# Routing in groups of three, three and two rows, the first a lap sooner, and an opening in another order

## The reference, cut to what matters

```
# 1. encoder, d = 128
x = emb[tokens]; x = x + scan(x @ W_upd + b)(decay, mask = token != 0) @ W_f + b_f
x = ln(x) * g + b
for i in range(4): x = x + gelu(ln(x) @ W1[i] + b1[i]) @ W2[i] + b2[i]
h = x @ head_W + head_b                                   # 64 wide
# 2. linear attention on layernorm(h), 4 heads of 32, softmax of k over the sequence, of q over 32
h = h + rmsnorm((context @ softmax(q)) @ w_out + b_out) * g_out + layernorm(h)
# 3. mixture of 8 experts on layernorm(h) (a second layernorm inside)
logits = xn @ Wr + br                                     # 8 wide
w = softmax of the two largest logits, 0 for the other six (first index wins a tie)
h = h + layernorm... + sum_e w_e * (gelu(xn @ W1[e] + b1[e]) @ W2[e] + b2[e])
```

## Time and profile before

| what | us |
|---|---|
| median of 3 runs | 427.89 (425.44 to 429.58) |
| profiled execution, own time | 426.03 |
| its span, first to last instruction | 424.2 |
| mean granted TensorE clock | 0.991 |
| busy: PE / DVE / ACT / POOL | 388.5 / 351.3 / 326.5 / 269.2 |
| VectorE idle for ScalarE's high parts in the layers | 25.2 |
| DMA, mean | 35 GB/s |

### The profile page before, as it was taken

One profiled execution on the slowest core, in us unless ns is written; L12 is line 12 of the kernel. 1 busy time (PEld: TensorE's weight loads), 2 busy tenths in 40 slices (PEclk: granted clock), 3 DMA queues, 4 the chain that ended last, 5 costly groups with the idle time before them and its releaser, 6 DMA issues.

```text
span 424.2 us, 6301 instructions
## 1 busy us (share of the span) xinstructions
PE 388.5 (92%) x1977; PEld 312.4 (74%) x1977; DVE 351.3 (83%) x820; ACT 326.5 (77%) x558; POOL 269.2 (63%) x435
## 2 busy tenths in 40 slices
PE   4797879999999999999999989888887988999995
PEld 2586568888888888888888868677665756776883
DVE  3888689888898889888889889888777779989885
ACT  1254588999999998888977854667866989988994
POOL 0555787778777879778776556686434666435452
PEclk9699999999999999999999999999999999999999
DMA  6800011232212221222221000000000000000001
GB/s 211 338 2 0 1 24 29 50 51 51 40 35 51 50 53 26 50 51 50 37 39 50 2 0 2 1 2 2 0 0 2 0 2 13 12 15 12 14 13 25
DMA packets 15849, 14.94 MB, mean 35 GB/s; under 512 B 9796, under 2 KB 10568, under 8 KB 15560
## 3 DMA queue, kind: packets, MB, share of 16 engines
q1 hardware_dynamic: 15816, 14.54, 13.9%
HBM read 13.42 MB, written 1.11 MB: 34 GB/s over the span
## 4 chain that ended last, share of the span: by engine, by line
PE 63%; DVE 17%; ACT 13%; issue 4%; POOL 2%; DMA 1%; SPq 0%; DVEq 0%; ACTq 0%
PE ps L1439 56%; PE ps L1462 4%; ACT hid L869 4%; ACT w_all L875 3%; ACT ezf L804 2%; DVE hid L1381 2%; DVE hh L1232 1%; DVE stats L949 1%; PE ps L1470 1%; DMA xn<-in_w_f 1%; DVE x L1381 1%; ACT scratch L865 1%; ACT scratch L769 1%; ACT hid_lo L825 1%; DVE xn_lo L1388 1%
## 5 line engine op out<-in xcount | busy, mean ns | idle before, releaser
L683 ACT ACTIVATE hid<-ps,b_fold 128x512 f32<-128x512 f32 x128 | 84.0, 681 | 21.2 <-PE ps L1439 20.8
L1023 DVE TENSOR_TENSOR hid_lo<-hid,hid_hi 128x1024 fp32r<-128x1024 f32 x64 | 78.6, 1228 | 25.4 <-ACT hid_hi L688 25.2
L1439 PE MATMUL ps<-xn_hi,w_all 128*128 128x512 f32 x256 | 87.5, 403 | 0.6 <-DVE xn_lo L1018 0.6
L1439 PE MATMUL ps<-hid_hi,w_all 128*128 128x512 f32 x256 | 85.0, 393 | 0.0
L688 ACT ACTIVATE hid_hi<-hid 128x1024 fp32r<-128x1024 f32 x64 | 67.9, 1061 | 2.0
L1439 PEld LDWEIGHTS ps<-xn_hi,w_all 128*128 128x128 f32 x256 | 48.4, 189 | 10.8 <-issue 0.9
L1439 PEld LDWEIGHTS ps<-hid_hi,w_all 128*128 128x128 f32 x256 | 48.1, 188 | 9.9
L1439 PE MATMUL ps<-xn_lo,w_all 128*128 128x512 f32 x128 | 49.9, 390 | 0.0
L1439 PE MATMUL ps<-hid_lo,w_all 128*128 128x512 f32 x128 | 49.8, 389 | 0.0
L869 ACT ACTIVATE hid<-ps,eb_fold 128x512 f32<-128x512 f32 x64 | 44.1, 688 | 0.2
L1439 PE MATMUL ps<-hid_hi,ew 128*128 128x512 f32 x128 | 41.8, 409 | 1.1 <-ACT hid L869 0.8
(11 more groups left out here) (229 smaller groups left out, 895.6 us busy)
## 6 DMA issues: line engine op xcount, KB each, us to landing
rstd_row<-roots SPq DMA_DIRECT2D x29, 256.0 KB, 4.1
hh<-in_tokens SPq DMA_DIRECT2D x8, 256.0 KB, 7.8
hid<-in_w SPq DMA_DIRECT2D x1, 1024.0 KB, 7.1
rstd_row<-in_w SPq DMA_DIRECT2D x1, 1024.0 KB, 10.2
out<-hh SPq DMA_DIRECT2D x7, 128.0 KB, 2.0
ew_raw<-in_expert_w SPq DMA_DIRECT2D x1, 512.0 KB, 9.9
roots<-rstd SPq DMA_DIRECT2D x29, 2.0 KB, 1.4
ew_raw<-in_expert_w SPq DMA_DIRECT2D x1, 256.0 KB, 10.0
```

What stands on the lines that cost most here:

```text
L683: act.activation(hid[:, j % 2, f, :], bank[f], ACT.Gelu, bias=b1_fold[:, j // B * F + f:j // B * F + f + 1]).then_inc(gelu_done, 1)
L1023: dve.tensor_tensor(hid_lo[:, j % 2, 2 * p:2 * p + 2, :], hid[:, j % 2, 2 * p:2 * p + 2, :], hid_hi[:, j % 2, 2 * p:2 * p + 2, :].bitcast( ...
L1439: return pe.matmul(out, lhsT, rhs, start=start, stop=stop)
```

## The change

Groups become rows 0 to 2, 3 to 5, 6 and 7. Group 0's logits and first maximum move from lap -2 to the end of lap -3, the rest to lap -2, its gates are turned and copied in lap -1 ahead of the context of row 7 (with a wait for the queries and values, whose banks they use). Groups 1 and 2 have their hots and second maximum in units 4, 6 and 7 of laps 1 and 3, weights and gates in units 1 and 2 of the lap behind, and every later row's gates are turned and copied a unit later. In the opening, one-hot of row 7 goes to POOL, three broadcasts move ahead of bias and expert products, and twelve matmuls of the clock-keeping kind are added.

```diff
-POOL_ROWS = (3, 4, 5)
+POOL_ROWS = (3, 4, 5, 7)
-GROUPS = ((0, 4), (4, 2), (6, 2))
-GROUP_OF = (0, 0, 0, 0, 1, 1, 2, 2)
+GROUPS = ((0, 3), (3, 3), (6, 2))
+GROUP_OF = (0, 0, 0, 1, 1, 1, 2, 2)
@@ POOL, opening
-            for n in POOL_ROWS:
+            for n in POOL_ROWS[0:3]:
                 one_hot(n)
             pool.wait_ge(mhalf_set, 1)
             inverse_root_of_pair(0)
+            one_hot(POOL_ROWS[3])
             inverse_root_of_pair(2)
@@ ScalarE, attention laps
                 if c >= 0:
                     k_turned(c, c % 2)
+                if m == -1:
+                    copy_gates(0)
                 if a < B:
                     exp_k(a, a % 2)
-                if m == -1:
-                    act.preload_act_table(ACT.Gelu)
...
                 if a + 2 < B:
                     z_hi(a + 2, a % 2)
-                if m == -1:
+                if m == -2:
+                    act.preload_act_table(ACT.Gelu)
                     gate(0)
...
-                if m == -1:
-                    copy_gates(0)
                 if a < B:
                     copy_v(a, a % 2)
@@ ScalarE, expert loop
-                if u == 3 and m in (2, 4):
-                    gate(m // 2)
-                if u == 5 and m + 1 < B:
+                if u == 7 and m in (1, 3):
+                    gate((m + 1) // 2)
+                if u == 6 and m + 1 < B:
                     copy_gates(m + 1)
@@ VectorE, opening
-                if n in (2, 3):
-                    one_hot(n + 4)
+                if n == 2:
+                    one_hot(6)
@@ VectorE, attention laps: first_hot, second_max, second_hot, weights and gates_out of group 0
-                if m == -1:
+                if m == -2:
...
+                if m == -3:
+                    take_logits(0)
                 if m == -2:
-                    take_logits(0)
-                if m == -1:
                     v = weights(0, v)
                     gates_out(0, v)
-                if m == -2:
+                if m == -3:
                     v = first_max(0)
@@ VectorE, expert loop, laps 1 and 3
                     if u == 3:
                         v = first_max(p)
+                    if u == 4:
+                        v = first_hot(p, v)
+                    if u == 6:
+                        v = second_max(p, v)
+                    if u == 7:
+                        v = second_hot(p, v)
@@ VectorE, expert loop, laps 2 and 4
-                    if u == 0:
-                        v = first_hot(p, v)
+                    if u == 1:
+                        v = weights(p, v)
                     if u == 2:
-                        v = second_max(p, v)
-                    if u == 3:
-                        v = second_hot(p, v)
-                    if u == 5:
-                        v = weights(p, v)
-                    if u == 6:
                         gates_out(p, v)
@@ TensorE, opening
             look_up(1)
+            keep_clock_at(0, bank[5])
+            keep_clock_at(0, bank[5])
...
                 if n + 1 < B:
                     look_up(n + 1)
+                if n in (4, 5):
+                    broadcast(n - 4, n - 4)
                 if n <= 4:
                     keep_clock_at(n, bank[5])
...
                 if 3 <= n < 3 + L:
                     bias_fold(n - 3)
+                if n == 6:
+                    broadcast(3, 3)
...
-                if n in (4, 5, 6):
-                    broadcast((0, 1, 3)[n - 4], (0, 1, 3)[n - 4])
...
                     turn(x[:, n - 5, :], x0_ready, n - 4, place_ffn(n - 5))
+                if n in (5, 6):
+                    keep_clock_at(n, bank[5])
@@ TensorE, turn_gates
+                if b == 0:
+                    pe.wait_ge(qsub_ready, B)
+                    pe.wait_ge(v_ready, B)
@@ TensorE, attention laps
                 if c >= 0:
                     k_transposes(c, c % 2)
+                if m == -1:
+                    turn_gates(0)
...
                     hidden(1)
-                    turn_gates(0)
                 if a + 1 < B:
                     queries_and_values(a + 1, (a + 1) % 2)
-                if m == -2:
+                if m == -3:
                     logits(0)
@@ TensorE, expert loop
-                if u == 4 and m + 1 < B:
+                if u == 5 and m + 1 < B:
                     turn_gates(m + 1)
```

More of the change, by code:

```diff
@@ L1478, in look_up @@
                 else:
-                    pe.wait_ge(onehot_dve, 1 + n - len(POOL_ROWS) * (n > POOL_ROWS[0]))
+                    pe.wait_ge(onehot_dve, sum(k not in POOL_ROWS for k in range(n + 1)))
                 if n >= 2:
```

## The result

The changed kernel is slower: 429.68 us at the median of 21 runs (426.99 to 432.72) against 426.45 for the kernel before in 21 runs beside it (425.36 to 430.99). The ratio is 1.0061, with a 95% interval of 1.0039 to 1.0083, so about +2.6 us; the two medians are 3.2 apart. The forecast was -1.6 us. The profiled executions differ by more, 428.0 against 424.2 us of span: +3.8. TensorE's mean granted clock in them is 0.987 and 0.991.

A forecast was written before the change was run, and what follows sets the result against it. TensorE was taken as the bound, with VectorE full in laps 2 and 4. Opening -0.5, lap 3 at +0.4 (attention's -0.5 included), laps 3 and 4 -1.5 gave -1.6 us: 426.3 from the median 427.89, range 422.5 to 430.2.

The forecast's parts named there:

- Opening: Before the layers: broadcast wait removed, VectorE free for the transposes, full clock possibly held; -0.3 to -0.7 us, taken as -0.5.
- signs of being wrong: Laps 1 and 2 together changing by more than 2 us, or layers starting over 1 us sooner or later than 46.95.
- End of attention: Up to the first expert job: new 3.4 us VectorE wait, yet job at 323.0 instead of 323.58; -0.5 us (-0.9 to +0.5).
- TensorE's new waits: End of attention: waits for queries and values of row 7 were claimed to end before the gates do.
- Laps 1 and 2: Expert loop: earlier routing of rows 3 to 5 costs +1.4 us on lap 1's chain, 0.5 recovered in lap 2.
- Stalls I priced in: Lap 1: steps waiting out POOL's 1.29 us subtraction; chain +0.85 us without stalls, +2.9 with two, taken as +1.4.
- Laps 3 and 4: Expert loop: 2.05 us of VectorE steps for rows 6 and 7 move into lap 3; gain 0 to 3.0, taken as 1.5.
- work for both laps: Laps 3 and 4: VectorE's work sums to 20.9 us without stalls, 23.9 with three, against 23.83 taken.
- Rival 1: Expert loop: every routing step at an even unit waits out POOL's subtraction; +1.4 to +2.4, 429.3 to 430.3 us; chance 0.20.
- the six steps it named: Routing steps predicted to stall beside POOL: units 4 and 6 of laps 1 and 3, unit 2 of laps 2 and 4.
- Rival 3: End of attention: VectorE's 3.4 us wait not recovered, first job 2.5 us later, rest as forecast; 429.4 us; chance 0.08.
- Lap -1's own slack is 2.06: End of attention: argument against the rival that VectorE's new 3.4 us wait is not recovered.

The follow-up runs named there:

- e1: Kernel before with only the opening's edits (one-hot of row 7 on POOL, three broadcasts earlier, twelve clock-keeping matmuls): 426.1 us, ratio to before 0.9956.
- e2: Changed kernel with the opening of before, so the routing edits alone: 429.22 us, ratio to before 1.0046.
- e14: Kernel before with only the opening's moves (one-hot and broadcasts), without the added clock-keeping matmuls: 426.37 us, ratio to before 1.0010.
- e5: Kernel before with only the expert loop's new placement of routing steps, groups of four, two and two kept: 428.19 us, ratio to before 1.0038.
- e3: Changed kernel with twelve more clock-keeping matmuls in lap -2, filling TensorE's pause of 3.25 us: 428.69 us, ratio to before 1.0043.
- e10: Changed kernel with second_max and second_hot of rows 3 to 5 behind row 7's output and moments in lap 1: 431.83 us, ratio to before 1.0067.
- e6: Changed kernel with the expert loop's routing steps moved off the even units: 429.76 us, ratio to before 1.0048.
- e11: Changed kernel with the edits of e4, e9 and e10 together: 426.91 us, ratio to before 0.9995.
- e7: Changed kernel with the edits of e4 and e6 together: 427.61 us, ratio to before 1.0002.
- e8: Kernel before with the opening's edits and its own late routing moved to odd units of laps 2 and 4: 426.53 us, ratio to before 0.9995.
- e9: Changed kernel with the routing of rows 6 and 7 put back into lap 4: 429.34 us, ratio to before 1.0041.
- e4: Changed kernel with group 0's take_logits, first_max and first_hot moved behind the subtraction of lap -2: 427.0 us, ratio to before 0.9986.
- e13: Kernel before with only the opening's added clock-keeping matmuls, without the moves: 427.44 us, ratio to before 1.0021.

## Why the prediction was wrong

The change was to save 1.6 us and costs 2.6. The absolute forecast of 426.3 stood on the first three runs of the kernel before, whose median (427.89) is 1.4 above that of 21 runs; that the median of 429.68 lies inside the range of 422.5 to 430.2 is luck of that base.

**Opening, forecast -0.5.** Right in kind, but smaller: the clock held, VectorE's broadcast wait went, the transposes kept their place. In the profiled pair it is -0.2 from the tables on (-0.4 with e1). It also tripped one of my signs of being wrong, since the layers began 1.06 us sooner; 0.86 of that is the tables. The clock was at 0.50 from 14.1 to 20.9, longer than the 14.3 to 20.1 I had read. By the Trainium skill (TensorE: Matmul & The Clock Gate, What's actually happening) the six matmuls keep the full clock, since activity releases the throttle. The traces agree: none of the 12 profiled executions with them falls at 14, and three of the four without them do (before, e2 and e14; e5 does not). They don't keep it for long: e3 and e10 fell at 31 to 36 and e6 at 21 to 25.

**End of attention, forecast -0.5, measured +3.2.** The new wait is 3.31 us where I wrote 3.4, and the moments of lap -2 were done at 313.1, sooner than my 314.2. The step that failed is "TensorE's new waits (for queries and values of row 7) end before the gates do". I followed VectorE's queue and costed TensorE's idle time at nothing, since the gates came later, and I named another wait than the one that came. The masked context of row 6, 5.9 us behind the late addition in that queue, holds TensorE for 3.25 us, and what TensorE did next ran at half clock for 10.2 us: 2.7 us in this execution, by e3, and 0 to 0.5 in the four other profiled executions with the same pause. Had the clock held, 303.34 + 19.73 = 323.07 would have been the first job, and my 323.0 with it. Even that is luck and hides an error of about 1 us, since my number was made for an opening that ended 1.06 later: counted from the layers' start it is +0.5 at full clock (e3), where I forecast -0.5. The wait alone costs more, 2.0 us (e3 against e11); the new grouping wins 1.5 of them back. The earlier trace rows had shown me a pause and a drop in the opening, and I didn't ask what a new pause of the same size would do elsewhere.

**Laps 1 and 2, forecast +0.9, measured +0.96.** The number is right, and one part of its chain: TensorE's wait on row 7's output grew from 0.44 to 1.39. In part it is luck: lap 1 grew by 2.2 us and lap 2 fell by 1.3, where I expected lap 1 "a little longer" and 0.5 recovered in lap 2. Stalls I priced in are there (1.25 and 0.74 us for first_hot and second_max). What they cost isn't shown: e6 and e7, with these two gone and others left, take 0.5 us less.

**Laps 3 and 4, forecast -1.5, measured +0.53.** Lap 4 came to 11.28, as I said (near 11). Lap 3 came to 13.08, where I said 11.5. The step that failed is "work for both laps: 2 x 8.35 + 4.2 = 20.9 without stalls": it adds up VectorE alone. The column beside it in the earlier trace rows has TensorE busy 10.18 of 10.18 and 13.07 of 13.65, which leaves 0.58 us to gain in both laps, whatever VectorE does, unless TensorE's work moves to another lap. (e8 gained 0.60 there, and paid 1.3 in lap 2.) I had called VectorE the full engine of lap 4, 13.10 of 13.65; TensorE stood 0.03 behind it. Moving VectorE's steps from lap 4 to lap 3 moved TensorE's work the same way. e5 shows it with the old groups (24.33), and e9, which puts the steps back, gets 0.2.

**The rivals.** Rival 1 gave 429.3 to 430.3, and the median is 429.68. That is in part luck of the base: as a difference it gave +1.4 to +2.4, and it allowed 1.0 at most for the end of attention, which came to +3.2 in the profile. Five of the six steps it named were stretched (1.25 and 0.74 in lap 1, 0.91 and 1.01 in lap 3, 0.72 in lap 4); the sixth, in unit 2 of lap 2, took 0.25, and one it did not name took 1.36. Whether they cost the +1.5 us of the loop stays open: e8, with no stall, gained nothing, and in e7 a stall of 1.30 stands in front of a wait of 1.76. By the Trainium skill (SBUF — State Buffer, SBUF: two separate sides) the shared pair is an exclusive lock, and VectorE's steps wait out POOL's; the trace agrees with the lock (steps of 1.36 and 1.25 us that end with POOL's of 1.28 and 1.29), and says nothing of a price.

Rival 3, given 0.08, is nearest to what the profile shows: the new wait dominates, with the first job 2.2 us later where it said 2.5; but its "rest as forecast" did not come. "Lap -1's own slack is 2.06" spoke against it, and that was no slack: in the kernel after VectorE still stands 2.12 us before its first expert job, now for ScalarE.

## What to carry to other kernels

Where two engines are each over 95% busy in a stretch, sum the idle time of the one that can't lose work, not the work of the one you relieve: TensorE's 0.58 us idle was about the most that laps 3 and 4 could give (the best order tried gave 0.60, and took more from lap 2). When a change lets an engine wait earlier in its queue, list who waits for the items behind it, and if TensorE then pauses for some microseconds, price what follows at 1.2 GHz, too: a range, since here it came to 0, 0.5 or 2.7 us behind the same pause. A stall that can be seen has no price yet; look for idle time behind the stalled instruction, on its engine and on the one that waits for it. Check an experiment that is to remove stalls for the new ones it makes (e7), before its time is read as their price.

## What the runs showed of the hardware

The granted clock fell to 0.50 in 15 of the 16 profiled executions before 420 us (e11_best is the exception), for 3 to 11 us each time, at few places: 14 to 25, 30 to 36, 254 to 265, 278 to 282, 308 to 321 and 386 to 390. At most of them TensorE had just waited or run short work. The pause of 3.25 us was followed by a fall in all five executions that have it. The pause of about 2.05 us before 253 to 256 was followed by one in seven (e1, e4, e6, e7, e8, e9, e13) and by none in the eight others that have it, so a pause of that size makes a fall possible and does not decide it; what does stays open. The granted clock goes with most of the scatter between runs: in 128 runs of the same kernel the correlation of span and clock is -0.84, and the line between them moves the span by about 7 us from 0.974 to 1.000.
